# Attention over 1600 tokens: tiles of 125 tokens instead of 100 for the projections, written out turn by turn

## What is computed

```python
x = x + self_attention(layernorm(x))    # 16 query heads, 4 key/value heads of 128; per-head layer norm and rotary tables on q and k; causal
x = x + cross_attention(layernorm(x), ctx)   # 32 heads of 16; rms norm on q and k
x = x + ffn(layernorm(x))               # 512 -> 2048 (silu(up) * gate) -> 512, ternary weights
```

## Time and profile before

| what | value |
|---|---|
| time, median of 3 runs | 1445.12 us (1444.58 to 1445.48) |
| the profiled execution's own time | 1444.46 us |
| its span | 1442.6 us |
| TensorE busy | 1383.5 us, 96% |
| VectorE busy | 843.9 us, 59% |
| ScalarE busy | 650.5 us, 45% |
| GpSimd busy | 308.0 us, 21% |
| the chain that ended last | 90% TensorE, 5% VectorE, 3% issue |

### The profile page before, as it was taken

The page is one execution under the profiler, slowest core; times in us unless marked ns, Lnnn a source line. Parts: engine busy times, 40 slices in busy tenths (PEclk is TensorE's granted clock), DMA queues, the critical chain, the costliest instruction groups (busy, mean ns, idle before and its releaser), DMA issues.

```text
span 1442.6 us, 31737 instructions
## 1 busy us (share of the span) xinstructions
PE 1383.5 (96%) x11512; PEld 895.8 (62%) x11512; DVE 843.9 (59%) x2080; ACT 650.5 (45%) x1452; POOL 308.0 (21%) x296
## 2 busy tenths in 40 slices
PE   7799999999999999799999999999999788999997
PEld 6566666666666666556666666666666544555554
DVE  5977777777777777734444444454544687444433
ACT  3533333333333333436666666666666422232322
POOL 0244444444444444211111111111121000000000
PEclk9899999999999999999999999999999999999999
DMA  9200000000000000311111111211111440000000
GB/s 330 71 1 0 0 0 0 0 0 0 0 0 0 0 0 1 129 54 56 43 42 42 42 42 51 74 44 42 42 42 52 176 146 1 24 0 23 0 24 24
DMA packets 22283, 58.44 MB, mean 41 GB/s; under 512 B 1272, under 2 KB 9464, under 8 KB 19036
## 3 DMA queue, kind: packets, MB, share of 16 engines
q1 hardware_dynamic: 22236, 57.81, 12.1%
HBM read 54.53 MB, written 3.28 MB: 40 GB/s over the span
## 4 chain that ended last, share of the span: by engine, by line
PE 90%; DVE 5%; issue 3%; ACT 1%; DMA 1%; POOL 0%; DVEq 0%; SPq 0%; ACTq 0%; POOLq 0%
PE A L1407 21%; PE A L1326 17%; PE A L1377 12%; PE C L1631 9%; PE C L1431 6%; PE B L1448 5%; PE C L1364 3%; PE C L1345 3%; PE A L1646 2%; PE B L1646 2%; PE B L1416 2%; PE B L1337 2%; PE B L1357 1%; PE C L1304 1%; DVE qk L977 1%
## 5 line engine op out<-in xcount | busy, mean ns | idle before, releaser
L1407 PE MATMUL A<-wxh,arena 128*122 128x512 f16 x768 | 198.1, 381 | 0.0
L1631 PE MATMUL C<-arena 128*128 128x400 f16 x1024 | 185.3, 335 | 5.1 <-DVE arena L978 5.0
L1326 PE MATMUL A<-arena,xh 128*100 128x512 f16 x768 | 181.6, 379 | 2.6 <-DVE arena L1043 1.8
L1377 PE MATMUL A<-arena,stageb 128*100 128x512 f16 x768 | 175.8, 379 | 0.7 <-ACT arena L557 0.7
L391 POOL TENSOR_TENSOR region<-tb,ub 100x512 f32<-100x512 f32 x80 | 101.7, 1271 | 308.6 <-DVE ub L828 308.6
L414 POOL TENSOR_TENSOR arena<-arena,region 100x512 f32<-100x512 f32 (+1 forms) x64 | 66.0, 1063 | 425.7 <-DVE region L941 425.7
L1631 PEld LDWEIGHTS C<-arena 128*128 128x128 bf16 x1024 | 100.6, 98 | 79.9 <-issue 8.6
L510 ACT ACTIVATE region<-C,negm 100x100 f32<-100x100 f32 x256 | 84.4, 348 | 138.8 <-DVE negm L867 138.8
L573 ACT ACTIVATE arena<-C 122x1600 f32<-122x1600 f32 x96 | 144.4, 1504 | 4.6 <-PE C L1431 2.6
L1326 PEld LDWEIGHTS A<-arena,xh 128*100 128x100 f16 x768 | 94.4, 125 | 69.9 <-issue 3.2
L1377 PEld LDWEIGHTS A<-arena,stageb 128*100 128x100 f16 x768 | 94.0, 125 | 62.8 <-ACT arena L557 1.1
(11 more groups left out here) (173 smaller groups left out, 2270.0 us busy)
## 6 DMA issues: line engine op xcount, KB each, us to landing
stageb<-in_wffn SPq DMA_DIRECT2D x16, 768.0 KB, 4.7
arena<-in_ctxt SPq DMA_DIRECT2D x16, 722.0 KB, 4.6
stageb<-in_wffn SPq DMA_DIRECT2D x6, 1024.0 KB, 4.9
arena<-in_wqkv SPq DMA_DIRECT2D x4, 1024.0 KB, 14.7
out_x<-xres SPq DMA_DIRECT2D x16, 200.0 KB
arena<-in_wx SPq DMA_DIRECT2D x3, 1024.0 KB, 8.3
wxh<-in_wffn SPq DMA_DIRECT2D x3, 1024.0 KB, 5.0
wxl<-in_wffn SPq DMA_DIRECT2D x3, 1024.0 KB, 4.8
```

The lines of the kernel that those rows point to most:

```text
L1326: ins = pe.matmul(A[j % 2][0:S, :], xp[:, k, :], wp[:, j, k, :], start=(n == 0), stop=(n == 11))
L1377: ins = pe.matmul(A[0][0:S, :], ap[:, h, :], wohl[:, g, part, h % 4, :], start=(n == 0), stop=(n == 47))
L1407: ins = pe.matmul(A[(par + n) % 2][0:rows, :], lhs, wp[:, 0 if n == 0 else 1 if n < 4 else 2, k, :], start=(i == 0), stop=(i == 11))
L1631: ins = pe.matmul(C[2 * (e % 2) + half][:, 0:UB * S], wf[:, 3 * (e // 4) + half, k, (e % 4) * 128:(e % 4 + 1) * 128], part[:, k, :], start ...
```

## The change

Tokens are now cut into 13 tiles: twelve of 125 and one of 100 (`TW`, `TL`, `rows_of`). The keys and queries are projected by tile, and so are the norms, the output projection, the transposes of the input and of the results, and the residual adds. The values, the scores and the softmax stay by batch of 100, and so does cross attention but for its inputs' norm and its results. Four tiles are five batches. So of five turns of self attention four project a tile (`whole`) and one does not (`attention_only`); the output projection is made in four of five as well. The fourth of five (b = 3, 8, 13) projects its whole tile and ends there; the fifth (b = 4, 9, 14) makes an output projection with the transposes of the fourth's tile inside it, and only then turns the probabilities. The first turn has no output projection and the last (b = 15) has two. The turned keys and queries of a tile belong to two batches, so `z_back` writes each group in two pieces, to two buffers. The inputs' high and low parts are rings of four tiles, the attention's output is a ring of two.

All hardware loops are gone: every turn is written out on every engine. 44 matmuls of one column at the start (`FILL`) are gone. The rotary tables are now made for 125 rows and four offsets, from a larger load. Of the output weights, part j = 9 may be made on ScalarE only after VectorE's `w_lo(8)` (the count 4 of `d_wlo`). Feed-forward has units of 375, 375, 375 and 475 tokens.

```diff
 ET = FE // 128
 
-FILL = 44
...
 
 def constants():
...
+def groups(b):
+
+    if b == NB - 1:
+        return []
+    p, r = divmod(b, 5)
+    return [(4 * p + r + 1, j) for j in range(5)] if r < 4 else []
+
+
+def z_tile(b):
+
+    p, r = divmod(b, 5)
+    return None if r == 3 or b == NB - 1 else 4 * p + (r + 1 if r < 3 else 4)
+
+
+def x_tile(b):
+
+    p, r = divmod(b, 5)
+    i = None if r == 3 else 4 * p + (r + 2 if r < 3 else 5)
+    return i if i is not None and i < TL else None
+
+
+def o_tile(b):
+
+    p, r = divmod(b, 5)
+    i = {0: 4 * p - 1, 1: 4 * p, 2: 4 * p + 1, 3: -1, 4: 4 * p + 2}[r]
+    return i if i >= 0 else None
...
+def unit_tiles(u):
+
+    return range(3 * u, 3 * u + 3 if u < 3 else TL)
...
                     act.wait_ge(pe_cen, 2 * (j - 3))
-                if j == 9:
-                    act.wait_ge(d_wlo, 1)
-                dst = wqh[:, j] if j < 6 else wohl[:, j - 6, 0] if j < 10 else wxh[:, j - 10]
+                elif 8 <= j < 10:
+                    act.wait_ge(d_wlo, {8: 1, 9: 4}[j])
+                elif j == 10:
...
+
+                n = rows_of(i)
+                dve.wait_ge(*count("pe_zT", i, j + 1))
+                z = bank[:, 0:4 * n].rearrange("p (h s) -> p h s", h=4)
+                for b, lo, hi, at in pieces(i):
+                    if j == 0 and b > 1:
+                        dve.wait_ge(*count("pe_s", b - 2, 4))
+                    c = ropeC[:, 0 if j == 0 else 1, lo:hi].unsqueeze(1).broadcast_to([128, 4, hi - lo])
+                    ins = dve.tensor_tensor(qks[b % 2][:, j, :, lo:hi], z[:, :, at:at + hi - lo], c, ALU.add)
+                    if b < last_batch(i):
+                        st.did(ins)
+                ins.then_inc(sig["d_zT"], 1)
...
+            def turn(b):
+                new = groups(b)
                 row_max(b, (0, 1))
                 row_max(b, (2, 3))
-                if first:
+                if b == 0:
                     w_lo(8)
+                if not new:
+                    sums(b, 0)
+                    back(b, 0)
+                    sums(b, 1)
+                    back(b, 1)
+                    if x_tile(b) is not None:
+                        x_lo(x_tile(b), A[1])
+                    sums(b, 2)
+                    back(b, 2)
+                    sums(b, 3)
+                    back(b, 3)
+                    add_attn(o_tile(b), A[0])
+                    back(b, 4)
+                    for g in range(4):
+                        a_lo(b, g)
+                    return
                 for g in range(4):
-                    proj(b + 1, g)
+                    proj(*new[g])
                     sums(b, g)
-                    if first and g == 1:
+                    if b == 0 and g == 1:
                         w_lo(9)
-
-                if last:
-                    wait(dve, "d_x1", 0, 1)
-                row_stats(0 if last else b + 2, ssq[:, 20:21])
-                proj(b + 1, 4)
+                next_stats(b)
+                proj(*new[4])
                 a_lo(b, 0)
-                head_norm(b + 1)
-                if last:
...
+            def project(i, j):
                 for xp, wp in ((xh, wqh), (xh, wql), (xl, wqh)):
                     for k in range(KT):
-                        ins = pe.matmul(A[j % 2][0:S, :], xp[:, k, :], wp[:, j, k, :], start=(n == 0), stop=(n == 11))
+                        ins = pe.matmul(A[j % 2][0:m, :], xp[:, k, at:at + m], wp[:, j, k, :],
+                                        start=(n == 0), stop=(n == 11))
                         n += 1
-                ins.then_inc(sig["pe_qkv"], 1)
...
-            def project_out(b, between=None):
-                n = 0
-                pe.wait_ge(d_wlo, 5)
+            def project_out(i, b, bank, between=None):
+
+                m, at, n = rows_of(i), i % 2 * TW, 0
                 for g in range(4):
                     if between and g > 0:
                         between(g - 1)
-                    wait(pe, "a_ahi", b, g + 1)
-                    wait(pe, "d_alo", b, g + 1)
+                    if last_batch(i) == b:
+                        pe.wait_ge(*count("a_ahi", b, g + 1))
+                        pe.wait_ge(*count("d_alo", b, g + 1))
                     for h in range(4 * g, 4 * g + 4):
                         for ap, part in ((ah, 0), (ah, 1), (al, 0)):
-                            ins = pe.matmul(A[0][0:S, :], ap[:, h, :], wohl[:, g, part, h % 4, :], start=(n == 0), stop=(n == 47))
+                            ins = pe.matmul(bank[0:m, :], ap[:, h, at:at + m], wohl[:, g, part, h % 4, :],
+                                            start=(n == 0), stop=(n == 47))
...
+                z_turn(z_tile(b), j, B[j % 2])
+
+            def whole(b):
+
+                i, o = groups(b)[0][0], o_tile(b)
                 for g in range(4):
                     scores(b, g)
-                for j in range(4):
-                    project(b + 1, j)
-                p_turn(b, 0)
-                project(b + 1, 4)
-                p_turn(b, 1)
+                pe.wait_ge(*count("d_xlo", i, 1))
+                if b < 2:
+                    pe.wait_ge(*count("d_u", i - 1, 5))
+                else:
+                    pe.wait_ge(*count("d_x1", o_tile(b - 1), 1))
+                project(i, 0)
+                if b % 5 == 0:
+                    pe.wait_ge(*count("a_v", b, 1))
+                project(i, 1)
+                for j in (2, 3):
+                    pe.wait_ge(*count("d_u", i, j - 1))
...
+                pe.wait_ge(*count("d_u", i, 4))
+                values_of(b + 1)
+                if z_tile(b) is None:
+                    return
 
                 def between(g):
-                    z_turn(b + 1, g)
-                    if g == 1 and not last:
-                        x_turn(b + 2)
-
-                project_out(b, between)
-                z_turn(b + 1, 3)
-                z_turn(b + 1, 4)
...
+                i, x, o = z_tile(b), x_tile(b), o_tile(b)
+                for g in range(4):
+                    scores(b, g)
+
+                def between(g):
+                    if g < 2:
+                        pe.wait_ge(*count("a_pT", b - 1, 3 + g))
+                    else:
+                        pe.wait_ge(*count("d_zT", i, g - 1))
+                    heads_back(b, g)
+                    if g == 1 and x is not None:
+                        pe.wait_ge(*count("a_v", b, 1))
+                        x_turn(x, A[1])
+
+                pe.wait_ge(*count("d_u", i, 5))
+                project_out(o, b, A[0], between)
+                for j in (3, 4):
+                    pe.wait_ge(*count("d_zT", i, j - 1))
+                    heads_back(b, j)
+                pe.wait_ge(*count("d_zT", i, 5))
+                p_turn(b, 0, B[0])
+                p_turn(b, 1, B[1])
+                attend(b, 0)
+                pe.wait_ge(*count("a_pT", b, 1))
+                p_turn(b, 2, B[0])
```

More of the change, by code:

```diff
@@ L16 @@
 NB, S, DM = 16, 100, 512
+TW = 125
+TL = 13
 KT = DM // 128
@@ L456, in turn @@
                         .then_inc(g_sum, 1)
-            two_ways(pool, turn)
+            for b in range(NB):
+                turn(b, b % 2, max(0, b - NB + 3))
         @block.scalar
@@ L1112, in turn @@
-                z_back(b + 1, 4)
-                if last:
-                    w_lo(10)
-            turn(0, first=True)
-            dve.wait_ge(ld_x, 16)
-            with dve.Fori(0, NB - 3) as i:
-                st.begin(i, 28)
-                turn(i + 1)
-            st.end(NB - 3)
-            turn(NB - 2, last=True)
+                if z_tile(b) is None:
+                    return
+                for j in range(4):
+                    back(b, j)
+                    if j == 1:
+                        x_lo(x_tile(b), A[1])
@@ L1125, in _ @@
+                if o_tile(b) is not None:
+                    add_attn(o_tile(b), A[0])
+                back(b, 4)
+            turn(0)
+            dve.wait_ge(ld_x, 16)
+            dve.wait_ge(ld_x2, 16)
+            for b in range(1, NB - 1):
+                turn(b)
             b = NB - 1
             row_max(b, (0, 1))
+            row_max(b, (2, 3))
+            sums(b, 0)
+            sums(b, 1)
+            w_lo(10)
+            sums(b, 2)
+            sums(b, 3)
+            x2_lo(0, A[1])
@@ new lines, in _ @@
+            pe.wait_ge(*count("a_v", 0, 1))
+            x_turn(1, A[1])
+            for j in range(5):
+                if j >= 2:
+                    pe.wait_ge(*count("d_zT", 0, j - 1))
+                z_turn(0, j, B[j % 2])
+            for b in range(NB - 1):
+                if groups(b):
+                    whole(b)
+                else:
+                    attention_only(b)
+            b = NB - 1
+            for g in range(4):
+                scores(b, g)
+            pe.wait_ge(*count("d_x1", TL - 3, 1))
```

1198 lines of the change are left out of this document (664 added, 534 removed).

## The result

The changed kernel takes **1402.2 us** (median of 4 runs, 1401.27 to 1403.94), the kernel before 1445.3 beside it: a ratio of 0.9696, 95% interval 0.9671 to 0.9721. The forecast was 1380.5 with a range of 1368 to 1398. The direction was right and the size was not: 43 us came of the 65 that were forecast, and the time lies 4 us outside the range. The profiled execution took 1401.41 us over a span of 1399.3; the forecast for it was 1379.8, so 21.6 us have to be found.

A forecast was written before the change was run, and what follows sets the result against it. TensorE was taken as the bound (busy 96%), except VectorE around feed-forward unit 0. Terms -59.6 - 1.0 + 0.2 - 3.6 - 0.7 = -64.7 took 1444.46 to 1379.8; the median being 0.7 higher gave 1380.5 us, range 1368 to 1398.

The forecast's parts named there:

- Start and first turn: Up to the end of the first self-attention turn: larger tables and a later weight copy, turn ending at 98.9, -1.0 us.
- the moved wait of `w_hi(9)`: First turn: ScalarE's last weight copy waits for VectorE's w_lo(8), so proj starts at 75.1 instead of 69.70, +5.4 us.
- Turns 1 to 14: Self attention: eight whole turns at +0.52 us each, three fourth-and-fifth pairs at -21.26 each, sum -59.6 us.
- Whole turns: Self-attention turns with projection and output projection: 35.65 us each instead of 35.13, without a gap.
- The pair: Fourth and fifth turn of five: 49.0 us instead of 70.26, with waits of 1.3 for a_lo and 1.7 for z_back.
- More waiting: Rival, 0.19: VectorE's chain later in fourth and fifth turns, 3 us idle plus 1.3 each, 3 more in first turn: 1396.
- Last turn: Last self-attention turn: one output projection covers the wait for weights, another stands at the end, +0.2 us.
- Cross attention: Cross attention: three of 16 result transposes fall away, -3.6 us.
- Feed-forward: Feed-forward: unit 0 -3.6, units 1 and 2 -7.9, unit 3 +12.0, tail +0.4, transposes -1.6; sum -0.7 us.
- The tail: End of feed-forward: wider copies, +0.4 us.
- Loops written out: All loops: removing the branch back gives 0, and fetching straight code costs 0.
- stream stalls: Rivals: instruction fetch transfers stall, at 0.15 us each 1404 (0.07), or at 0.45 us each 1452, slower than before (0.03).

The follow-up runs named there:

- the new order of the pair: Changed kernel, VectorE only: a_lo(1) to a_lo(3) ahead of the input's norm in fourth turns, residual add behind the last z_back in fifth turns: 1393.29 us.
- the five: Changed kernel with 128-row tables and first x tile, w_hi(9) behind the second square, stores of 120 and 5 rows, VectorE's reordered fourth and fifth turns: 1373.92 us.
- the six edits together: Changed kernel with 128-row tables and first x, w_hi(9) later, split stores, VectorE's fourth and fifth turns reordered, four tiles in feed-forward unit 0: 1360.7 us, ratio 0.9404.
- the units' order: Changed kernel with four input tiles (500 columns) in feed-forward unit 0 and 350 columns in the last unit: 1389.48 us, median of three runs.

## Why the prediction was wrong, point by point

- **Start and first turn, the step that failed.** "The larger table load and tables cost VectorE 3 us, of which I let 0.5 reach TensorE": it was 10.97. I priced the load by its bytes. What decided was its row count, which spread it over 5 of 16 DMA engines, held up SyncE's issues and slowed the weights beside it; the clock then added 1.5. This step alone is 11.2 of the 21.6 us. The rest of it was right, in part by luck: with tables of 128 rows the first `proj` is at 23.94, ScalarE's fourth weight copy at 70.55 (forecast 71), the first exponentials at 72.37 (73) and turn 1 at 99.11 (98.9). But of the 5.4 us for the moved wait of `w_hi(9)` the wait itself made only some 3.1: TensorE stood still for 4.94 us, and three waits of the kernel before in that turn, 1.85 together, fell away. Another 2.6 are the clock's, which the forecast did not have: the 24 matmuls behind the wait took 7.98 instead of 5.39 us.
- **The row count of a transfer** was in no term. The packets above show 10 engines for 100 rows, 5 for 125, 15 for 120, and the share of 0.06 with 127 rows shows 1. The Trainium skill (DMA: Bandwidth & Descriptors, Why a DMA increments its semaphore by 16 and not by 1) says that a transfer is split over the largest number of engines up to 16 that divides the size of its slowest dimension, with 10 for 100 rows and 1 for 127 as examples; the trace agrees in all four counts. By it a tile of 125 rows is a poor transfer wherever one is on the path, and the prediction did not weigh it.
- **Turns 1 to 14.** Whole turns right to 0.04 us. The pair was right in each of its two waits (1.20 for 1.3, 1.66 for 1.7), and the sum of the three was 2.3 us too low: the first two came 1.6 and 1.7 over the forecast, by the clock, and the third 1.0 under it, since it has less to turn (no input tile is left, and the keys and queries are those of the tile of 100) and waits 1.40 us instead of 1.66. "More waiting" had this price, 1.3 a pair, but tied it to 3 us of idle at a stretch; here 1.20, 1.66 and 0.25 us had gone ahead of it.
- **Last turn.** 47.6 us, forecast 47.2.
- **Cross attention.** Forecast -3.6, measured -1.2 (499.5 us before and 498.4 after, from its first scores at 641.87 and 595.48 to unit 0). Twelve turns in its middle took 379.4 us against 12 x 31.82 = 381.8, so 15 such spans bring 3.1: the term was nearly right. The rest is the clock again: the projection at 596.99 took 4.45 us, before 2.6. It stands behind three short waits (0.97, 0.97 and 0.55 us), but the kernel before has nearly the same there (0.97, 0.97 and 0.37) and its clock stayed up (1.00), so why it fell is not shown.
- **Feed-forward.** Unit 0 -3.7 (forecast -3.6), units 1 and 2 together -8.6 (forecast -7.9, and a part of -1.6 for transposes), unit 3 up to its last turn back +12.3 (forecast +12.0). The tail was the miss, forecast +0.4, measured +4.2, and the same cause as the start: stores of 125 rows on 5 engines (in two pieces they gave 4.6 us of the tail back).
- **Loops written out.** Right: nothing that can be told, shown by the kernel before without its loops. The "stream stalls" rivals fall with it.
- **The 44 one-column matmuls** that are gone had no term, and no run tests them alone. The traces show little: from the input's transposes behind them to the first scores it was 7.3 us before and 7.7 after, with wider transposes and writes, and the scores took 4.06 and 4.12 us.
- **The sum:** 11.2 + 2.3 + 0.4 + 2.4 + 4.9 = 21.2 of 21.6 us. Some 13 of them go back to the row count of transfers (9.5 at the start, 3.8 in the tail), some 7 to the clock (1.5 at the start, 3.3 in the pairs, 1.8 in cross attention). The 128-row tables and the split stores show the first part. For the clock, the new order of the pair shows 3.3 us of it, and what made it fall in cross attention stays open.

## What to carry to other kernels

A tile size is also the row count of its transfers: read off the trace how many DMA engines carry one (small packets per transfer, or the share of 16), and pad the rows or split them before you change a tile from 100 or 128 to 125. A short wait on a saturated TensorE can cost the clock as well: taking 1.8 us of waits out of a pair gave 3.4 in two of three pairs, so let the range hold more than the length of such waits. Where an engine idles in one stage and not in others, put the widest unit of work there.

## What was not expected of the hardware

- A transfer confined to one or five DMA engines is not only late itself. SyncE's issues behind it took up to 14.71 us, and transfers beside one of 125 rows ran at 242 instead of 422 GB/s with all engines counted as busy. The kernel before shows a milder case beside its own loads of 100 rows (295 GB/s from 20 to 24 us, at a share of 1.02). The second part has no cause here. The Trainium skill (DMA: Bandwidth & Descriptors, The descriptor swizzle) says that in a transfer of 128 rows each engine writes one port of its own; whether other row counts slow their neighbours through shared ports, no run here shows.
- TensorE's clock fell inside both of the first two pairs with waits of 1.20, 1.66 and 0.25 us, and in none of the six such pairs with 1.06 and 0.25 (the pair's order, the five and the six edits together). But the waits alone do not decide: of the 18 first and second pairs in the nine kernels with the old order, 17 had a clock of 0.93 or 0.97, and one had the same waits and 1.00 (the first with `w_hi(9)` moved).
- The third pair of the same code took 48.0 us in the changed kernel, with a clock of 1.00, and 49.5 with 0.97 in four kernels that differ from it elsewhere (x as 128 rows, stores in two, tables in two, the units' order). Each is one execution, and runs of one kernel lie up to 5.5 us apart (1395.91 to 1401.39 with the tables' wait moved), so whether the edit or the execution decides is not shown. A gain of 1 or 2 us is therefore read at its place in the trace and not from the time.
